# One core of Trainium2: order of the first batch, fills of TensorE and the adds of a convolution moved in a two-part block kernel

## The reference

```python
n = layernorm(x)
q, k, v = split(n @ Wqkv)                      # per head
# 11 offsets 0, 1, 2, 4 ... 512: key and value that many tokens back
sc = einsum('bhsd,bhskd->bhsk', q, k[pos - offsets]) / sqrt(d)
tele = einsum('bhsk,bhskd->bhsd', softmax(sc), v[pos - offsets])
conv = causal_depthwise_conv(v, conv_w)        # 7 taps
fq, fk = elu(q) + 1, elu(k) + 1                # linear attention
low = fq @ (fk^T v) / (fq . sum(fk) + 1e-6)
x = x + layernorm(n + (tele + conv + low) @ Wo)
# feed-forward: 8 experts, 2 of them chosen by sigmoid(x @ gate_W), and a shared one
n = layernorm(x)
g = renormalised top 2 of sigmoid(n @ gate_W) * route_scale
y = sum_e g_e * (gelu(n @ W1_e + b1_e) @ W2_e + b2_e) + gelu(n @ Ws1 + bs1) @ Ws2 + bs2
out = x + layernorm(y)
```

## Time and profile before

| | us |
|---|---|
| median of three runs | 297.0 (296.45 to 302.2) |
| the profiled execution | 296.57 |
| its span, first to last instruction | 294.7 |
| TensorE busy | 248.8 (84%) |
| VectorE busy | 231.7 (79%) |
| ScalarE busy | 198.2 (67%) |
| GpSimd busy | 94.7 (32%) |

### The profile page before, as it was taken

One profiled execution on the slowest core, in us unless ns is written; L12 is line 12 of the kernel. 1 busy time (PEld: TensorE's weight loads), 2 busy tenths in 40 slices (PEclk: granted clock), 3 DMA queues, 4 the chain that ended last, 5 costly groups with the idle time before them and its releaser, 6 DMA issues.

```text
span 294.7 us, 4732 instructions
## 1 busy us (share of the span) xinstructions
PE 248.8 (84%) x1593; PEld 173.7 (59%) x1593; DVE 231.7 (79%) x598; ACT 198.2 (67%) x461; POOL 94.7 (32%) x152
## 2 busy tenths in 40 slices
PE   5857978886989699979988699979969699899893
PEld 5413774884625377858625377758526578774383
DVE  6699798489997848889889757999589699627653
ACT  2475465637969768849977777939876747476841
POOL 5920161028272124044562024053531131430023
PEclk9997997999899799989999799979999999999999
DMA  7437989300689943500899934201799863000003
GB/s 197 110 97 233 225 190 201 75 0 2 181 232 191 233 83 71 146 0 4 241 230 223 183 77 93 53 1 33 241 215 225 191 122 73 1 1 2 0 14 95
DMA packets 24258, 35.27 MB, mean 120 GB/s; under 512 B 4053, under 2 KB 17198, under 8 KB 24234
## 3 DMA queue, kind: packets, MB, share of 16 engines
q1 hardware_dynamic: 20346, 21.59, 25.7%
q0 software_dynamic: 3888, 13.37, 25.3%
HBM read 5.07 MB, written 2.10 MB: 24 GB/s over the span
## 4 chain that ended last, share of the span: by engine, by line
PE 47%; DVE 22%; ACT 18%; POOL 7%; issue 4%; DMA 1%; POOLq 0%; DVEq 0%; ACTq 0%
DVE prods L282 10%; PE psH L1365 7%; PE psF L1424 7%; PE psA L1271 6%; PE psY L1462 6%; POOL rstd L483 4%; PE psA L1462 3%; PE psA L1333 2%; ACT xn L597 2%; DVE x L1068 2%; POOL var L481 2%; PE psG L1462 2%; PE psA L1263 1%; PE psG L1448 1%; ACT L691 1%
## 5 line engine op out<-in xcount | busy, mean ns | idle before, releaser
L282 DVE TENSOR_TENSOR prods<-qT,kT 128x1024 f32<-128x1024 f32 (+1 forms) x48 | 50.7, 1112 | 7.2 <-PE psA L1333 5.0
L483 POOL TENSOR_TENSOR rstd<-var,neg_half 128x4 f32<-128x4 f32 (+2 forms) x28 | 41.2, 1472 | 2.3
L1365 PE MATMUL psH<-ident,prods 128*128 128x128 f32 x324 | 39.9, 273 | 0.0
L481 POOL TENSOR_SCALAR var<-ss 128x4 f32<-128x4 f32 (+1 forms) x25 | 10.2, 407 | 91.6 <-ACT squares L765 35.3
L1365 PEld LDWEIGHTS psH<-ident,prods 128*128 128x128 f32 x324 | 36.4, 141 | 2.3 <-issue 2.3
L1037 DVE TENSOR_TENSOR prods<-v_shift,prob 128x896 f32<-128x896 f32 x32 | 34.7, 1085 | 0.0
L1424 PE MATMUL psF<-x3T,w 128*128 128x512 f32 x58 | 29.0, 611 | 1.0 <-ACT hid L741 0.6
L1333 PE MATMUL psA<-prods,slot_sel 128*32 128x512 f32 x168 | 24.3, 627 | 3.7 <-DVE prods L282 2.4
L1271 PE MATMUL psA<-xnT,wqkv 128*128 128x512 f32 x36 | 22.1, 752 | 5.5 <-ACT xnT L586 5.5
L1150 DVE TENSOR_TENSOR hid<-hid,psG 128x512 f32<-128x512 f32 x32 | 20.8, 683 | 6.3 <-PE psG L1448 5.7
L741 ACT ACTIVATE hid<-psF,b1c 128x512 f32<-128x512 f32 x29 | 19.1, 688 | 8.8 <-PE psF L1424 8.7
(11 more groups left out here) (241 smaller groups left out, 583.5 us busy)
## 6 DMA issues: line engine op xcount, KB each, us to landing
v_shift<-v_tok SPq DMA_DIRECT2D x20, 448.0 KB
convT<-tapT POOLq DMA_DIRECT2D x8, 512.0 KB, 5.7
x_res<-L_attn_x SPq DMA_DIRECT2D x4, 512.0 KB, 10.0
tapT<-tapT POOLq DMA_DIRECT2D x4, 512.0 KB, 10.9
out<-y_out SPq DMA_DIRECT2D x7, 256.0 KB, 3.9
x_in<-L_attn_x SPq DMA_DIRECT2D x3, 512.0 KB, 4.9
v_shift<-v_tok SPq DMA_DIRECT2D x4, 384.0 KB
convT<-kexp POOLq DMA_DIRECT2D x3, 512.0 KB, 10.3
```

The lines of the kernel that those rows point to most:

```text
L282: return eng.tensor_tensor(prods[:, QUADS * (s % 2) + q, t0:t1], qT[:, t0:t1], kT[:, PRE - off + t0:PRE - off + t1], ALU.mult)
L481: nc.gpsimd.tensor_scalar(var[:, cols], src, scale, EPS, ALU.mult, ALU.add).then_inc(step, 1)
L483: return nc.gpsimd.tensor_tensor(rstd[:, cols], var[:, cols], neg_half[:, cols], ALU.pow)
L1365: ins = pe.matmul(dst, terms[:, j % TERM_BUFS, m, :], ident[:], is_transpose=True, start=False, stop=(m == live[-1]))
```

## The change

On TensorE, in the first batch: 18 fills ahead of the first score sums, 26 ahead of the turned keys, 16 instead of 20 ahead of the third group, 24 instead of 10 ahead of the terms; the query projection of batch 1 behind the first term; the wait for the centred weights at the first output. In the steady batches: 18 fills ahead of the key projection, 14 ahead of the second output, 12 instead of 10 in the last batch; `low` ahead of `gates_expert_major`; the last expert tile of a unit behind the first score sums of the next batch. On ScalarE: the first four taps ahead of the copies of the turned keys, the other three ahead of the scores; tap 6 beside taps 4 and 5. On VectorE: `stats(1)` ahead of the linear state, the centring behind the fourth weighed tile, `add_conv(b, 1)` ahead of `residual(2b)`. On GpSimd: `first_conv_sums` ahead of `ln1(1)`.

```diff
--- before.py
+++ after.py
@@ -47,9 +47,9 @@
 SLOTS, QUADS = 3, 4
 TERM_BUFS = 4
 WARM_UP = 20
-FIRST_FILL_SUM, FIRST_FILL_X, FIRST_FILL_TERMS = 20, 40, 10
+FIRST_FILL_HEADS, FIRST_FILL_FK, FIRST_FILL_SUM, FIRST_FILL_X, FIRST_FILL_TERMS = 18, 26, 16, 40, 24
 FILL_FRONT = 5
-FILL_LAST = 10
+FILL_LAST, FILL_K, FILL_OUT = 12, 18, 14
 CH = 5
 
 
@@ -557,6 +557,8 @@
                 attn, ffn, more = b < B, b >= 1, b < B - 1
                 u0, u1 = 2 * b - 2, 2 * b - 1
                 if attn:
+                    if b == 0:
+                        first_conv_sums()
                     if more:
                         ln1(b + 1)
                     if b >= 2:
@@ -568,8 +570,6 @@
                         sum_taps_third(b)
                         ln4(u0)
                         add_residual(u0)
-                    else:
-                        first_conv_sums()
                     ln2(2 * b)
                     ln3(2 * b)
                     ln2(2 * b + 1)
@@ -780,8 +780,9 @@
             key_parts(0)
             token_major_v(0)
             query_parts(0)
+            scale_first_taps(range(0, 4))
             token_major_fk(0)
-            scale_first_taps(range(0, 4))
+            scale_first_taps(range(4, TAPS))
             for b in range(B + 1):
 
                 attn, ffn, more = b < B, b >= 1, b < B - 1
@@ -789,13 +790,11 @@
                 if attn:
                     if ffn:
                         gate_logits(u0)
-                        scale_taps(b, range(4, 6))
+                        scale_taps(b, range(4, TAPS))
                         if more:
                             normalise1(b + 1, range(0, TPH))
                         norm3_squares(u1)
                     scores(b)
-                    if b == 0:
-                        scale_first_taps(range(4, TAPS))
                     if ffn:
                         if more:
                             normalise1(b + 1, range(TPH, NT))
@@ -812,7 +811,6 @@
                     if ffn:
                         normalise3(u1)
                         evacuate_x3(u1)
-                        scale_taps(b, range(6, TAPS))
                         evacuate_shared(u1)
                         gate_logits(u1)
                     if more:
@@ -1186,10 +1184,10 @@
                             stats(b + 1)
                     products(b, 2, range(0, 1))
                     products(b, 2, range(1, 3), gate_step_of(u0, 0))
+                    if b == 0:
+                        stats(b + 1)
                     linear_state(b, gate_step_of(u0, 2))
                     if b == 0:
-                        stats(b + 1)
-                        centre_weights()
                         dve.wait_ge(consts_ready, 2)
                     if b >= 2:
                         finish(u0 - 1)
@@ -1210,13 +1208,15 @@
                                 gates(u1, range(2 * (3 * (j - 1) + n), 2 * (3 * (j - 1) + n + 1)))
 
                         weigh(b, j, two_gate_steps)
+                        if b == 0 and j == TPH - 1:
+                            centre_weights()
                         if ffn:
                             if j in (6, 7):
                                 gate_hidden(u1, range(2 * (j - 6), 2 * (j - 5)))
                         if j == TPH:
                             add_conv(b, 0)
+                    add_conv(b, 1)
                     residual(2 * b)
-                    add_conv(b, 1)
                     if more:
                         key_features(b + 1)
                 else:
@@ -1481,13 +1481,17 @@
                 if attn:
                     if b == 0:
                         token_major_v(b)
+                        keep_busy(FIRST_FILL_HEADS, psG[:, 1, :])
                         pe.wait_ge(consts_ready, 1)
                     sum_heads(b, 0)
                     if b == 0:
+                        keep_busy(FIRST_FILL_FK, psG[:, 1, :])
                         token_major_fk(b)
                         sum_heads(b, 1)
                     if ffn:
                         turn_logits(u0)
+                        if b >= 2:
+                            experts_out(u0 - 1, range(TPH - 1, TPH))
                     linear_state(b, b == 0)
                     if b:
                         sum_heads(b, 1)
@@ -1497,11 +1501,10 @@
                     if ffn:
                         hidden(u0, range(0, 2))
                     turn_scores(b)
+                    low(b)
                     if ffn:
                         gates_expert_major(u0)
-                    low(b)
                     if b == 0:
-                        pe.wait_ge(w_centred, 1)
                         keep_busy(FIRST_FILL_X, psG[:, 1, :])
                     if ffn:
                         hidden(u0, (2,))
@@ -1514,6 +1517,9 @@
                         keep_busy(FILL_LAST, psA[:, 0, :])
                     if ffn:
                         spread_gates(u0, range(2, 4))
+                    if more and ffn:
+                        pe.wait_ge(hidden_free, upto(u1, N_HIDDEN, -1))
+                        keep_busy(FILL_K, front(u1, X3))
                     if more:
                         project_k(b + 1)
                     else:
@@ -1527,7 +1533,6 @@
                         experts_out(u0, range(2, TPH))
                         hidden(u1, range(0, 2))
                     if b == 0:
-                        project_q(b + 1)
                         keep_busy(FIRST_FILL_TERMS, psG[:, 1, :])
                     for j in range(NT):
                         if ffn:
@@ -1537,11 +1542,16 @@
                                 gates_expert_major(u1)
                             if j in (5, 7):
                                 spread_gates(u1, range(j - 5, j - 3))
-                        if more and j == 1 and b:
+                        if more and j == 1:
                             project_q(b + 1)
                         sum_terms(b, j)
                         if j == TPH:
+                            if b == 0:
+                                pe.wait_ge(w_centred, 1)
                             output(b, 0)
+                    if ffn:
+                        pe.wait_ge(gated, upto(u1, 4, 4))
+                    keep_busy(FILL_OUT, psG[:, 1, :])
                     output(b, 1)
                     if more:
                         project_v(b + 1)
@@ -1553,8 +1563,8 @@
                             experts_out(u1, range(2, 3))
                         token_major_fk(b + 1)
                         gate_logits(2 * b)
-                    if ffn:
-                        experts_out(u1, range(TPH - 1, TPH) if more else range(TPH - 1))
+                    elif ffn:
+                        experts_out(u1, range(TPH - 1))
                 else:
                     spare = psA[:, 0, :]
                     turn_x3(u0)
```

## The result

The changed kernel took 307.77 us (median of four runs, 306.94 to 307.91) against 297.3 of the kernel before in the same runs: 1.0356 times, 95% interval 1.0323 to 1.039. It is slower, and 2.3 us above the upper end of the forecast's range (292 to 305.5 us around 301.6). The profiled execution took 307.72 us, its span is 305.9 (before 296.57 and 294.7).

The account below looks back on a forecast made before the run. The prediction took the first batch's chain to bound the kernel: ln1(1) on GpSimd, ScalarE's normalising, TensorE's turns, the sums of terms. 296.57 + 10.7 - 2.8 - 0.6 - 2.3 = 301.6 us, range 292 to 305.5.

Parts of the forecast that it names:

- the term of the first batch: First batch: ln1(1), moved behind the convolution adds on GpSimd, delays turns and first term; +10.7 us in total time.
- Adds land late: Rival at GpSimd's wait for first_sums[1]: landing at 49 or later, each us later costs one; 303.5 to 307 us, chance 0.14.
- They land at about 47: GpSimd, first batch: five adds, 2.62 MB at 0.121 MB/us beside the copies, take 21.7 us and land at about 47.
- ln1(1) in the same 3.48 us: GpSimd, first batch: after issuing the last add, ln1(1) takes 3.48 us as before, done at 51.8 instead of 42.30.
- Some 0.1 more: End of first batch: residual of tile half 0 follows the add of the convolution instead of hiding beside turns; 0.1 us more.
- until 48: SP queue, first batch: the shifted copies of v, sharing with the adds, last until 48 us instead of 41.
- The change does what its words say: Rival: all sums landed when GpSimd gets to ln1(1), first batch loses nothing; 289 to 291 us, chance 0.08.
- Adds land early: Rival: adds don't share with the copies, ln1(1) ends 4 us late instead of 9.5; 290 to 298 us, chance 0.15.
- The clock is not held: Rival: fills leave gaps and TensorE's clock still falls at the keys; 304.4 us, chance 0.07.
- The steady terms: Batches after the first: key fills -2.8 us, end of a batch -0.8 + 0.2, low-rank part ahead of turned gates -2.3.
- The zero for the first score sums: VectorE, steady batches: 1.41 us won at the first score sums is lost waiting for gate_logits' exponential; 0 in sum.
- the end-of-batch term: End of a batch: convolution add ahead of the residual and 14 fills before the second output; -0.8 + 0.2 us.

## Why the prediction was wrong, point by point

The step that failed is the term of the first batch, +10.7, which measured +16.9. Its mechanism held: ln1(1) waits behind landing adds, the turns behind ln1(1), the first term behind the turns. Its size was wrong in four places: a landing, ln1(1), the clock and the residual, +2.9, +0.85, +1.7 and +0.6, which with 0.15 at the hand-overs make the 6.2 us. The time lies above the range of the rival "Adds land late" too (303.5 to 307).

*"They land at about 47".* GpSimd goes on at 50.35 where the forecast had 47.4, +2.9. The bytes were right: 2.58 MB of adds had moved by 47, 705 packets beside 726. But a landing is the last packet's, and the last 15 packets took until 50 while 154 packets of copies moved. I worked with the mean rate of a queue and set no price on its end. That each transfer's sixteen engines finish apart and that only all of them together mean that it has landed, the Trainium skill says in "DMA: Bandwidth & Descriptors", section "Why a DMA increments its semaphore by 16 and not by 1"; the tail agrees with it, though no row here tells the engines apart. So far the rival "Adds land late" is what came: it decides from 49 on, and the landing was at 50. It had 0.14, and at a us for a us it gives 304.5; the other three places stood in no rival. That the company of the copies makes the landing late is shown by the run without them (6.0 us instead of 10.6), and the run without adds in DMA shows the reverse (copies done by 36 us, not 51). Two figures beside this step are wrong in themselves: a landing at 49 makes ln1(1) 11 us late, not "12 and more", and 5 MB in 14 us are 1.6 times the 0.22 MB/us, not twice. Neither enters the sum.

*"ln1(1) in the same 3.48 us".* It took 4.33 (51.28 to 55.61), +0.85. VectorE weighs its first tiles just then. In the run with 180 fills, again beside weighed tiles, the same four instructions took 3.93 us (51.82 to 55.75); beside VectorE's last steps of the softmax, in the run with the copies behind, 2.50 (40.77 to 43.27), and beside its centring, in the run with the early taps put back, 2.50 (53.51 to 56.01). So their time differs with what VectorE does beside them, but not simply (the 3.48 us of the kernel before were beside softmax steps too), no run changed that alone, and the cause stays open.

*The clock behind the wait.* From the turns to the first term the forecast has 6.7 us, the trace 8.38: +1.7. The text looked for stretches at 1.2 GHz at the keys and ends of steady batches and did not ask what an idle time of 14 us that it forecast itself would do (18.02 us came). With fills through the wait the first term came 2.46 us earlier (1.7 of it the miss, the rest what the forecast had allowed for a slow projection), and the run took 2.2 us less.

*"Some 0.1 more" at the residual.* From the first term to the key features 15.67 us, forecast 15.06: +0.6. The residual of the first batch used to run while TensorE summed the last term; behind the add of the convolution it starts only when that term is there (81.30, 81.91). The rows of the kernel before:

```profile
64.42 1.12 DVE L1068 SCALAR_TENSOR_TENSOR x<-psY,rstd,x_res 128x128 f32<-128x128 f32 x4 [1.29 <-POOL rstd L483]
65.46 0.68 DVE L1057 TENSOR_TENSOR prods<-psH,convT 128x512 f32<-128x512 f32 x1
```

From the sums of the last tile to the key features it was 2.40 us (63.66 to 66.06) and is 3.04 (79.90 to 82.94); with the end of a batch alone changed in the kernel before it is 3.05 (63.92 to 66.97).

The copies "until 48" ended at 50.97; harmless in the changed kernel, since TensorE came later, but with ln1(1) put back they hold the first term (51.98) and cost the clock behind it (296.6 us). "The change does what its words say" and "Adds land early" are refuted, and so is "The clock is not held", at the keys.

*The steady terms*, -5.7 in sum, came as -5.7 in the changed kernel, and batch by batch: the forecast's terms for the second, the third and the last batch (1.8, 2.1 and 1.8 us) measured 1.69, 2.51 and 1.48. One by one they did not come: -1.7, +3.8 and -3.9 alone (by the ratios) make -1.8 in sum, while the kernel with the first batch put back is 5.1 us faster by its ratio with a first batch 0.9 longer, so some -6. Why is not shown, and so it is open how much of the agreement is luck. One reading is that a fill that keeps the clock up in one place leaves the next idle times, and the clock then falls behind one of these (228.75 and 154.75 above), while with all fills in none is left at the keys and the ends of batches. But the clock also fell in different places behind the same code, and the moves of the expert tile and of tap 6, and the two more fills of the last batch, were not run alone. The forecast priced each stretch by its own fill, 1.4 us per stretch, which the trace of the fills alone shows too, but only for the batch in which they stand. The zero for the first score sums held in the third batch (batch 2 of the forecast): VectorE's products follow without a wait and its gate step waits for the exponential instead, as the rows below show. In the last batch both waits stand, 1.58 and 1.57 us, where the products waited 3.62 before.

```profile
157.99 2.33 DVE L282 TENSOR_TENSOR prods<-qT,kT 128x1024 f32<-128x1024 f32 x2
161.35 0.18 DVE L1089 TENSOR_SCALAR gtmp<-gexp 128x32 f32<-128x32 f32 x1 [1.03 <-ACT gexp L733]
```

Open is how the end-of-batch term splits in company: only its sum with the others is measured.

## What to carry to other kernels

An instruction that waits for a transfer is a wall on its queue: before moving it up, ask what stands behind it, and price the landing by the slowest landing measured beside the other traffic, not by the bytes at the mean rate. When one stage is bound by bytes that two queues move, starting one of them earlier can make the other late; keep the work that needs neither (here ln1, worth 11 us) ahead of the waits for them. Moving it further ahead won nothing here, because the landing of the adds then held the batch. A wait that a change creates can cost the clock behind it too. And measure fills with the others in place, over several runs: those at the end of a batch cost 3.8 us alone and stand in the fastest kernels of this case.

## What the runs showed of the hardware that was not expected

- Two queues took 705 and 726 packets in the same 22 us, and yet an add's last 0.04 MB took 3 us more; from its issue to GpSimd's next step it was 10.6 us beside copies and 6.0 without.
- A GpSimd add of 128x1024 f32 took 2.4 to 3.4 us, and VectorE's instructions that started beside it with two inputs in the on-chip memory some 2 us longer each (a fold of 0.22 us took 2.25), while the eight statistics of x, with one input, took 1.63 us beside it as without. Each of the slowed folds ended just behind the add beside it (at 38.41, 40.85 and 43.13; the adds at 38.01, 40.63 and 43.05). The Trainium skill, "GPSIMD Engine Reference", section "8. Key points", says that the two share their way to the on-chip memory and contend, among other cases, when a VectorE instruction has two inputs there; the products, which have two, agree (9.95 us for three instead of 3.48).
- An idle time of 2.44 us ahead of the same turn was followed by 1.2 GHz in one kernel and by 2.4 GHz in another, and the first score sums, with the same code ahead of them, ran at 1.2 GHz in one run and at 2.4 in another (3.64 and 1.92 us).
